# Writing the relative products of a sequence's first and last query block in four pieces of 32 rows

## The reference, cut to what matters

```python
dist = jnp.arange(s)[:, None] - jnp.arange(s)[None, :]
dist = jnp.clip(dist, -MAX_REL, MAX_REL) + MAX_REL          # MAX_REL = 128, s = 512
rel_pos = rel_emb[dist]
scores = jnp.einsum('bhqd,bhkd->bhqk', q, k)
scores = scores + jnp.einsum('bhqd,qkd->bhqk', q, rel_pos)
attn = jax.nn.softmax(scores / np.sqrt(HEAD_DIM), axis=-1)  # 16 heads of 8
```

## Time and profile before

| | us |
|---|---|
| median of 3 runs (lowest, highest) | 2944.68 (2943.84, 2947.04) |
| the profiled execution's own time | 2947.33 |
| its span, first to last instruction | 2945.5 |
| attention, about | 790 to 2195 |
| mean granted TensorE clock | 0.961 of full speed |

### The profile page before, as it was taken

The page is one execution under the profiler, slowest core; times in us unless marked ns, Lnnn a source line. Parts: engine busy times, 40 slices in busy tenths (PEclk is TensorE's granted clock), DMA queues, the critical chain, the costliest instruction groups (busy, mean ns, idle before and its releaser), DMA issues. The chain is left out here.

```text
span 2945.5 us, 60238 instructions
## 1 busy us (share of the span) xinstructions
PE 2752.1 (93%) x18624; PEld 1985.9 (67%) x18624; DVE 1893.1 (64%) x4781; ACT 1735.6 (59%) x3222; POOL 1392.2 (47%) x1728
## 2 busy tenths in 40 slices
PE   5999999999499999999999999999998999999999
PEld 4777777777255666566666565666656777777777
DVE  7666666667256666666666666666647666666665
ACT  4656566655256666556666555666646656665655
POOL 3555555555444344444434444444414555555554
PEclk9999999999689999999999999999998999999999
DMA  4000000000377788888878877887831000000000
GB/s 115 1 0 0 0 0 0 0 0 1 66 220 221 223 235 230 213 219 224 226 219 224 225 213 215 229 224 228 230 103 50 8 7 4 7 7 4 7 6 9
DMA packets 233801, 324.94 MB, mean 110 GB/s; under 512 B 29444, under 2 KB 188548, under 8 KB 233604
## 3 DMA queue, kind: packets, MB, share of 16 engines
q1 hardware_dynamic: 194436, 171.36, 24.5%
q0 software_dynamic: 36864, 150.49, 15.3%
q10 hardware_dynamic: 2304, 0.61, 0.1%
HBM read 141.68 MB, written 154.92 MB: 101 GB/s over the span
## 5 line engine op out<-in xcount | busy, mean ns | idle before, releaser
L1089 DVE CUSTOM_DVE_ANT_0 at_junk<-at_ps_s,at_rel 128x512 bf16<-128x512 f32 x1024 | 666.1, 688 | 403.9 <-PE at_ps_s L758 386.3
L895 ACT ACTIVATE at_probs<-at_ps_t 128x512 f32<-128x512 f32 x1024 | 558.7, 595 | 504.5 <-PE at_ps_t L743 504.3
L378 POOL TENSOR_TENSOR ffn_h_lo<-ffn_h,ffn_h_hi 128x512 fp32r<-128x512 f32 x384 | 502.1, 1311 | 475.6 <-ACT ffn_h_hi L305 475.6
L489 DVE TENSOR_TENSOR ffn_h<-ffn_silu,ffn_ps_gate 128x512 f32<-128x512 f32 x576 | 393.7, 683 | 406.7 <-ACT ffn_silu L348 404.4
L305 ACT CAST ffn_h_hi<-ffn_h 128x512 fp32r<-128x512 f32 x576 | 358.8, 623 | 408.4 <-DVE ffn_h L489 407.0
L194 PE MATMUL ffn_ps_mid<-ffn_xT_hi,ffn_w_mid 128*128 128x512 f32 x1152 | 480.2, 417 | 22.7 <-DVE ffn_h L489 11.5
L743 PE MATMUL at_ps_t<-tab_ident,at_rel 128*128 128x128 f32 x3328 | 497.1, 290 | 0.0
L194 PE MATMUL ffn_ps_gate<-ffn_xT_hi,ffn_w_gate 128*128 128x512 f32 x1152 | 456.7, 396 | 0.0
L194 PE MATMUL ffn_ps_out<-ffn_h_hi,ffn_w_out 128*128 128x512 f32 x1152 | 453.9, 395 | 0.2
L743 PEld LDWEIGHTS at_ps_t<-tab_ident,at_rel 128*128 128x128 f32 x3328 | 372.2, 146 | 82.3 <-issue 22.7
L348 ACT ACTIVATE ffn_silu<-ffn_ps_mid 128x512 f32<-128x512 f32 x576 | 343.8, 597 | 80.2 <-PE ffn_ps_gate L194 73.2
(11 more groups left out here) (161 smaller groups left out, 4000.2 us busy)
## 6 DMA issues: line engine op xcount, KB each, us to landing
at_band<-at_src POOLq DMA_DIRECT2D x256, 574.0 KB, 4.8
at_rel<-at_band SPq DMA_DIRECT2D x512, 143.5 KB, 3.8
at_qs<-at_q_hi SPq DMA_DIRECT2D x128, 64.0 KB
at_ks<-at_k_hi SPq DMA_DIRECT2D x128, 64.0 KB
at_rel<-at_band SPq DMA_DIRECT2D x64, 128.0 KB, 3.5
at_rel<-at_band SPq DMA_DIRECT2D x64, 127.5 KB, 3.1
at_rel<-at_band SPq DMA_DIRECT2D x64, 112.0 KB, 2.9
at_rel<-at_band SPq DMA_DIRECT2D x64, 111.5 KB, 3.5
```

The source lines that it names most:

```text
L378: pool.tensor_tensor(h_lo[:, u % RH, :], h[:, u % RH, :], h_hi[:, u % RH, :].bitcast(F32), ALU.subtract).then_inc(hlo_pool.sem, 1)
L489: dve.tensor_tensor(h[:, u % RH, :], silu[:, u % RH, :], ps_gate[:, u % 2, :], ALU.mult).then_inc(h_done.sem, 1)
L895: act.activation(probs[:, kp, 2 * hp + i].rearrange("p n q -> p (n q)"), ps_t[:, i, :], ACT.Exp).then_inc(exp_done.sem, 1)
L1089: dve.tensor_tensor_reduce(out=junk[:, i, :], in0=ps_s[:, i, :], in1=rel[:, c % RREL, l, h, :], scale=1.0, scalar=-3e38, op0=ALU.add, op1= ...
```

## The change

The DRAM write of the two edge blocks (query block 0, which is `l = 0` of an even item, and query block 3, `l = 1` of an odd item) becomes four DMAs of 32 rows. Piece g of block 0 writes the columns from 96 - 32g to 287, piece g of block 3 the columns from 0 to 255 - 32g. The two inner blocks are still written with one DMA. The waits count the DMAs sent so far.

```diff
+        def sent_pieces(c, l):
+
+            qb = 2 * half_of(c) + l
+            if qb == 0:
+                return [(32 * g, 32 * g + 32, P - 32 * g - 32, WIDE) for g in range(4)]
+            if qb == QPB - 1:
+                return [(32 * g, 32 * g + 32, 0, BAND - 1 - 32 * g) for g in range(4)]
+            return [(0, P, 0, WIDE)]
+
+        def sent_by(c, l):
+
+            return 16 * sum(len(sent_pieces(i, l)) for i in range(c + 1))
...
-                if hp == 0:
-                    band_out[l].wait(act, j, 0)
+                if hp == 0 and c > 0:
+                    act.wait_ge(band_out[l].sem, sent_by(c - 1, l))
...
-                pool.dma_start(heads[:, :, PAD:HEADW], src[:, l]).then_inc(band_out[l].sem, 16)
+                for lo, hi, first, last in sent_pieces(c, l):
+                    pool.dma_start(heads[lo:hi, :, PAD + first:PAD + last], src[lo:hi, l, :, first:last]).then_inc(band_out[l].sem, 16)
...
-                sp.wait_ge(band_out[l].sem, band_out[l].at(j, 16))
+                sp.wait_ge(band_out[l].sem, sent_by(c, l))
```

## The result

| | kernel before | changed kernel |
|---|---|---|
| median, us (lowest, highest; runs) | 2944.22 (2941.19, 2947.04; 6) | 2959.86 (2949.78, 2964.28; 6) |
| ratio, with 95% interval | | 1.0049 (1.003 to 1.0068) |
| profiled execution, its own time and span, us | 2947.33, 2945.5 | 2949.78, 2948.0 |

The change makes the kernel slower by 15.6 us, half a per cent. The forecast was 2955 us with a range of 2934 to 2985. The profiled execution of the changed kernel is the fastest of its six, only 2.5 us above the one before. So its trace shows where things moved, and the loss itself has to be read from the medians.

The account below looks back on a forecast made before the run. PE was taken as the bound, 93% busy, stalled in attention mainly by late `mrow`. Per sequence 0.3 + 0.45 - 0.1 = 0.65 us, times 16 = +10 us on the 2944.68 us median: 2955 us, range 2934 to 2985.

Parts of the forecast that it names:

- the sum of +10 us: Attention, 16 sequences: 0.3 + 0.45 us of stalls minus 0.1 us for saved bytes, 0.65 us each, made +10 us.
- 0.3 us at slot 63: Late fetches in slot 62 delay `mrow`: PE stalls about 0.3 us per sequence, ends 0 and 1.5.
- 0.45 us more at the start of slot 68: Slot 66's late fetches delay slot 67's `mrow`, lengthening PE's 3.31 us wait by 0.45 us, ends 0 and 1.2.
- Three more issues hold POOL, 1.9 us: On POOL, each edge block's three extra issues hold the line 0.63 us apiece, 1.9 us in all.
- The fetches start that much later and PE's stalls grow: SP's fetches in even slots start 1.9 us later; PE's `mrow` waits go from 23 to some 35, 55 to about 65 us.
- The landing of `mrow`: The row-maxima DMA, behind four fetches on SP's queue, was taken to need 2.8 us to land.
- Rival 4: Saved DMA time shortens slot 67's stall by 0.8 us, perhaps restoring the clock: 2870 to 2939 us, chance 0.12.
- the stall of 1.72 us: PE stall in the earlier trace, read as leaving the clock at 1.00, while one of 3.31 us left 0.50.
- What these stalls cost: PE's added waits for `mrow` in slots 62 and 67: 0.3 and 0.45 us for each of 16 sequences.
- Fewer bytes shorten the queue by 50 us: Band-write queue: 16.8 MB less, 50 us over 128 edge writes; worth 2 us of run time, ends 0 and 12.
- The write lands at the same time, so nothing: Block 0's write lands within 0.5 us of its former time; ACT has 0.49 us of slack, so no cost.
- the case against itself: Block 0's last piece takes the whole write's 3.8 us, landing 5.7 us after first issue, 0.6 us late: 7 us.

Follow-up runs that it names:

- the repeat on another chip: The changed kernel measured once more, unaltered, against the kernel before on its own chip: 2955.87 us, ratio 1.0037.
- uncut and narrow: Kernel before, with one write per edge block (block 0 columns 48 to 287, block 3 columns 0 to 207), some relative terms missing: 2939.61 us, ratio 0.9979.
- GpSimd held by three copies: Kernel before, writes uncut, with three small copies into an unused tile on GpSimd after each edge write: 2949.29 us, ratio 1.0013.
- the fill is out of the way: Changed kernel with the fill of odd items ahead of block 3's four writes instead of behind them: 2960.19 us, ratio 1.0057.
- run 217: Not a run number: 217 ns is a packet time in the changed kernel with all four pieces 287 columns wide, 2984.04 us, ratio 1.0126.

## Why the prediction came out as it did

The sign and the range held, and the sum of +10 us stands beside +15.6 and, in the repeat on another chip, +10.4. That the sum came so near is in good part luck: its two terms of stall (0.3 us at slot 63, 0.45 us more at the start of slot 68, which has slot 60's place in its sequence) are not there, the stalls that came instead cost less than their 12 us, and the rest is a cost that the prediction set to nothing.

- *Three more issues hold POOL, 1.9 us.* Right in kind. A piece holds it for 0.52 us, so 1.44 us, and the price is nearly fixed: a piece a quarter as large costs 0.52 against 0.63. The Trainium skill, "DMA: Bandwidth & Descriptors", "Anatomy of one DMA — SWDGE (gpsimd) path", calls descriptor generation small and says that many descriptors can be emitted before it shows; the trace agrees in the main, a quarter of the rows taking 0.11 us off 0.63. A piece of 64 rows lies between, at 0.57.
- *The fetches start that much later and PE's stalls grow.* Right: 23 waits became 37, 55 us became 65. But the places were wrong. The stall that I expected at the start of slot 63 did not come. The one before slot 60 shrank from 3.30 to 2.58 us where I expected it longer, and the new ones stand two slots on; in the sequence followed above, SP's queue has hardly a gap in front of it. The landing of `mrow`, taken as 2.8 us, was a part of this: in the 23 stalls of the kernel before PE starts 3.2 to 6.4 us after its issue, 5.1 in the median, and in the 37 of the changed kernel 3.0 to 6.4. Rival 4 had the clock that comes back with a shorter stall; it did not see that the time is given back two slots later. The prediction's reading that the stall of 1.72 us left the clock at 1.00 is right, but the stretch in the earlier trace rows ends with that stall; the stretch behind it, 1516.08 to 1520, has 1.00 too.
- *What these stalls cost.* The step that I over-sized. With the same delay and 37 stalls, but uncut writes, the kernel lost 0.13%, 4 us (at most 8.5) in place of the 12 us that slots 62 and 67 were to cost.
- *Fewer bytes shorten the queue by 50 us.* This step failed. The bytes do so only in an uncut write. Time of this queue: 451 us for 150.49 MB is 3.0 us per MB. Taking the inner blocks' half, 226 us, from each kernel (their packets took 225 us before and 221 to 223 in the kernels with four pieces), the edge blocks' 75.2 MB cost 3.0 us per MB uncut, and in four pieces of full width (505 - 226) / 75.2 = 3.7; in the change (445 - 226) / 58.5 = 3.7; in two pieces (475 - 226) / 62.7 = 4.0; uncut and narrow (402 - 226) / 58.5 = 3.0. Cutting spends what the narrower rows save, and that price of cutting is a term that the prediction had at nothing. The saved bytes alone are worth 6 us, where it took 2 (with 12 as the end); cutting alone costs 38. One caution: a queue's time holds what its packets lose to the other queue. The other one, with the same 171.36 MB in both, fell from 24.5% to 23.7%, by 23 us. Both together fell by 28 us, 1172 to 1144, uncut and narrow by 44 (24.7% and 13.7% of 2937.9 us), and rose by 22 with pieces of full width (23.1% and 16.9% of 2986.8 us). But both together are no steady measure: with GpSimd held by three copies they are 20 us below the kernel before (24.1% and 15.0% of 2945.6 us) though no DMA differs. So how much of the cost of cutting is added work and how much a shift between queues is not shown. The writes' own queue is steadier, 442 to 451 us in the five runs with uncut writes of full width, against 505. "Rules for kernel authors" on the same page of the Trainium skill advises against cutting a transfer in two by partitions, since the parts serialize on the same engines; the runs here agree and show a loss.
- *The write lands at the same time, so nothing.* Wrong. Block 0 lands 5.65 us after its first issue in place of 4.76. ACT needs the buffer after 5.1 us, and the prediction had named 5.7 us as the case against itself, and put it aside. ACT's waits grew by 13 us, by 7.5 us when only block 0 is cut, and PE's for ACT from 14.5 to 19.4 us; they grow further, to 31.9 us, when the fill is out of the way. At full width, where no saved bytes hide it, its growth is nearly a third of the 41 us of the account above.

What is shown: cutting costs 1.26% at equal bytes, of which GpSimd's time explains 0.13%; narrower pieces give 28 us of it back; the queue of the writes spends 3.7 us or more per MB on them in place of 3.0; and the slower writes reach PE by two waits, for the row maxima and for ACT's `src`; in the one pair of profiles with the same delay and the same bytes its busy time, with more of it at the lower clock, grew too. What stays open is how they divide in the change itself, where stalls, clock and SP's queue trade with one another from slot to slot and one profile of the changed kernel differs from the next by 4 us. Why a cut write moves fewer bytes per us is open too: each piece reads 32 or 64 of the 128 partitions, but no run here varied that alone.

## What to carry to other kernels

Price a cut write by its queue's time per MB, not by its bytes: here 3.7 us in place of 3.0 used up a saving of 22% on the edge blocks. When an issue is delayed, make the same delay with work that does nothing before calling it the cause; here it gave as many stalls as the change and an eighth of a per cent, where cutting at equal bytes cost ten times as much. When a buffer is freed by a DMA, count from the first issue to the last landing of all its pieces, against the moment at which the buffer is needed again. And where a stall in front of a slow-clock stretch shrinks, look further on for the place where the time is given back; in the slots followed here it was two slots later, behind a DMA queue with hardly a gap.

## What the runs showed of the hardware

A DMA issue on GpSimd cost nearly the same at the sizes measured: 711 ns for 574 KB, 585 ns in the median of 640 issues of which 512 are pieces of 80 to 144 KB. In the line of instructions it held GpSimd for 0.52, 0.57 and 0.63 us with 32, 64 and 128 rows. With a write cut into four pieces of 32 rows, its packets of 4592 bytes took 269 ns in the mean, those of uncut writes in the same run 217 ns. TensorE's granted clock fell to 0.50 behind stalls of 3.30 and 3.48 us and stayed at 1.00 behind stalls of 1.72 and 2.58 us, but it also fell behind one of 2.57 us: the length of a stall alone does not tell it.
